# Flamingo block on one core: other engine orders for the first two samples, gate scratch in PSUM, offsets on ScalarE, first context and first w in halves

## The reference

```python
# layernorm of x over its 1024 columns is inp_q; ctx is inp_k and inp_v
t = Wt @ ctx;  p = Wp @ layernorm(x);  g = Wg @ ctx          # 256x256 times 256x1024
att = sum(p * g) over each of 8 groups of 32 rows
y = groupwise Wz @ (att * t)
x1 = x + tanh(g_xattn) * (groupnorm(y) * gn_w + gn_b + ctx)
h = layernorm(x1)
scores = (h @ Wq.T) @ keys.T                                 # 64 experts
gate = softmax of the 16 largest scores, 0 elsewhere
z = h @ A.T                                                  # 512 columns, 8 per expert
out = x1 + tanh(g_ffn) * 2 * ((z * gate) @ B.T)
```

## Time and profile before

| what | us |
|---|---|
| median of three runs | 344.52 |
| profiled execution, its own time | 344.88 |
| span of the profiled execution | 343.1 |
| TensorE busy | 335.0 (98%) |
| VectorE busy | 253.6 (74%) |
| ScalarE busy | 155.2 (45%) |
| GpSimd busy | 155.6 (45%) |

### The profile page before, as it was taken

One profiled execution on the slowest core, in us unless ns is written; L12 is line 12 of the kernel. 1 busy time (PEld: TensorE's weight loads), 2 busy tenths in 40 slices (PEclk: granted clock), 3 DMA queues, 4 the chain that ended last, 5 costly groups with the idle time before them and its releaser, 6 DMA issues.

```text
span 343.1 us, 5733 instructions
## 1 busy us (share of the span) xinstructions
PE 335.0 (98%) x2108; PEld 304.0 (89%) x2108; DVE 253.6 (74%) x656; ACT 155.2 (45%) x254; POOL 155.6 (45%) x148
## 2 busy tenths in 40 slices
PE   8999997999999999999999999999999999999996
PEld 8587997789988999889988899889998899889984
DVE  0858999899688866897868975888668978685362
ACT  2489826873165622554234811656225542144110
POOL 0082999189354470654445381544706544001000
PEclk9999999899999999999999999999999999999999
DMA  8999603660642509052370606424090110002002
GB/s 274 406 394 399 237 1 104 265 214 33 197 171 67 181 6 332 32 166 82 86 283 0 220 29 201 168 71 176 8 330 32 63 62 2 1 0 108 16 32 92
DMA packets 14924, 47.50 MB, mean 138 GB/s; under 512 B 1824, under 2 KB 1952, under 8 KB 14896
## 3 DMA queue, kind: packets, MB, share of 16 engines
q1 hardware_dynamic: 14544, 46.93, 38.5%
q10 hardware_dynamic: 352, 0.20, 0.2%
HBM read 38.74 MB, written 8.39 MB: 137 GB/s over the span
## 4 chain that ended last, share of the span: by engine, by line
PE 86%; POOL 9%; issue 2%; ACT 1%; DVE 1%; POOLq 0%; DVEq 0%
PE z_ps L926 24%; PE w_ps L953 24%; PE w_ps L814 10%; PE w_ps L859 10%; PE t_ps L913 4%; PE z_ps L885 3%; PE w_ps L839 2%; PE z_ps L798 2%; PE w_ps L926 2%; PE w_ps L963 2%; PE t_ps L940 2%; POOL A_lo L267 2%; POOL cT_lo L260 2%; POOL xT_lo L260 1%; POOL B_lo L267 1%
## 5 line engine op out<-in xcount | busy, mean ns | idle before, releaser
L260 POOL TENSOR_TENSOR xT_lo<-xT_in,xT_hi 128x512 fp32r<-128x512 f32 x28 | 35.6, 1295 | 48.9 <-ACT xT_hi L358 46.1
L953 PE MATMUL w_ps<-B_hi,zT_hi 128*128 128x512 f32 x128 | 53.4, 417 | 1.8 <-DVE zT_lo L653 1.8
L953 PE MATMUL w_ps<-B_hi,zT_lo 128*128 128x512 f32 x128 | 51.0, 398 | 0.0
L953 PE MATMUL w_ps<-B_lo,zT_hi 128*128 128x512 f32 x128 | 50.7, 396 | 0.0
L926 PE MATMUL z_ps<-A_hi,hT_hi 128*128 128x288 f32 x224 | 48.5, 298 | 1.0 <-DVE hT_lo L648 1.0
L926 PE MATMUL z_ps<-A_lo,hT_hi 128*128 128x288 f32 x224 | 48.0, 296 | 0.0
L926 PE MATMUL z_ps<-A_hi,hT_lo 128*128 128x288 f32 x224 | 47.9, 296 | 0.0
L437 ACT ACTIVATE ex<-sc,neg_max 128x64 f32<-128x64 f32 x16 | 5.6, 349 | 74.6 <-DVE neg_max L663 74.6
L926 PEld LDWEIGHTS z_ps<-A_hi,hT_hi 128*128 128x128 f32 x224 | 36.3, 189 | 1.8 <-DVE hT_lo L648 1.2
L926 PEld LDWEIGHTS z_ps<-A_hi,hT_lo 128*128 128x128 f32 x224 | 36.1, 189 | 0.0
L260 POOL TENSOR_TENSOR cT_lo<-cT_in,cT_hi 128x512 fp32r<-128x512 f32 x28 | 36.0, 1308 | 0.0
(11 more groups left out here) (147 smaller groups left out, 802.3 us busy)
## 6 DMA issues: line engine op xcount, KB each, us to landing
c_sb<-in_ctx SPq DMA_DIRECT2D x16, 512.0 KB, 4.9
x_sb<-in_x SPq DMA_DIRECT2D x16, 512.0 KB, 7.3
xT_in<-in_xT SPq DMA_DIRECT2D x14, 512.0 KB, 6.7
cT_in<-in_cT SPq DMA_DIRECT2D x14, 512.0 KB, 7.7
out_block<-uw SPq DMA_DIRECT2D x14, 512.0 KB, 2.7
A_in<-in_aT SPq DMA_DIRECT2D x8, 256.0 KB, 12.8
B_in<-in_bT SPq DMA_DIRECT2D x8, 256.0 KB, 12.5
xT_first<-in_xT SPq DMA_DIRECT2D x2, 512.0 KB, 9.0
```

The costliest lines, as they stand in the source:

```text
L260: last = pool.tensor_tensor(lo[:, chunks, :], came[:, chunks, :], hi[:, chunks, :].bitcast(f32), ALU.subtract)
L953: last = pe.matmul(w_ps[k][:, :], z[:, t, row], w[:, j, cols], start=(j == 0 and z is zT_hi and w is B_hi), stop=(j == KN - 1 and z is zT_lo))
```

## The change

- TensorE: `keep_busy(24)` and `keep_busy(8)` become 12 and 4. `first_u` waits for ctx by column halves. In sample 0 the first half of `hT` waits only for the first half of w. `hT(0, 1)` and `hT(1, 1)` move: the one between `out_product(2, 0)` and `out_product(3, 0)`, the other into `z_product(0, 1)`.
- SyncE: ctx of sample 0 is loaded by column halves of both tiles.
- GpSimd: takes lots 0 and 1 ahead of `y_root(0)` and lots 14 and 15 after lots 8 to 11; gives lot 4 away. `x_root(1)` goes ahead of the lots of B, the two `w_root` move by one place or two.
- VectorE: gives lots 0, 1, 14, 15 and `offsets` away and takes lot 4; lots 2 and 3 lie in the wait for `y_root(0)`; w of sample 0 is made in four halves with `hT_low` of its first half between them; half of the row statistics of x of sample 1 lies ahead of `gate(0, 0)`; `x_stats(2)` goes ahead of `hT_low(1, 1)`. The group deviation loses one copy.
- ScalarE: makes the offsets (`offsets`) and for the first two samples a part of the variance (`u_variance`); all eight lots of B and `scale_ctx(1)` come ahead of `exps(1, 0)`.
- The gate's `ex` and `g_rec` lie in columns 288 to 352 of the second z bank in PSUM.

```diff
+        def z_banks(t, n):
+            return w_ps[NH:USES] if t == 1 and n in (0, NB - 1) else z_ps
+
+        def gate_space(t, n):
+            bank = z_banks(t, n)[1]
+            return bank[:, ZH:ZH + NE], bank[:, ZH + NE:ZH + NE + 1]
...
+            def load_first_c():
+                for h in range(NH):
+                    cols = slice(h * HALF, (h + 1) * HALF)
+                    sp.dma_start(c_sb[0][:, :, cols],
+                                 ctx[0].rearrange("t p d -> p t d")[:, :, cols]).then_inc(c_in[h], 16)
...
             x_add(0)
+            lot_low(0)
+            lot_low(1)
             y_root(0)
             pool.wait_ge(w_done, per_tile(0, T - 1))
-            for j in range(KH, KD):
+            for j in range(KH + 1, KD):
                 lot_low(j)
+            w_root(0)
             xT_low(0, 1)
-            w_root(0)
             cT_low(0, 1)
             xT_low(1, 1)
             cT_low(1, 1)
+            x_root(1)
             for j in range(KD, KD + KN):
                 lot_low(j)
-            x_root(1)
+            for j in range(KD + KN + 2, N_LOTS):
+                lot_low(j)
             x_add(1)
             y_root(1)
...
+            def u_variance(n):
+                act.wait_ge(mean_read, n + 1)
+                for t in range(T):
+                    act.activation(att_var[:, T + t:T + t + 1], u_dev[:, t:t + 1], ACT.Identity, scale=u_dev[:, t:t + 1],
+                                   bias=u_mv[:, t, 1:2]).then_inc(u_rows, 1)
+            def offsets(n):
+                act.wait_ge(w_done, per_tile(n, 0))
+                for t in range(T):
+                    act.activation(kappa0[:, t:t + 1], beta[:, t:t + 1], ACT.Identity, scale=-1.0,
+                                   bias=gnb_t[:, t:t + 1]).then_inc(kappa0_done, 1)
+                act.wait_ge(kappa0_done, per_tile(n, T - 1))
+                for t in range(T):
+                    act.activation(kappa[:, t:t + 1], u_dev[:, t:t + 1], ACT.Identity, scale=slope[:, t:t + 1],
+                                   bias=kappa0[:, t:t + 1]).then_inc(kappa_done, 1)
...
             exps(0, 0)
+            offsets(0)
             act.wait_ge(gram_done, per_tile(0, T - 1))
-            for j in range(KD, KD + KN):
+            for j in range(KD, N_LOTS):
                 lot_high(j)
+            scale_ctx(1)
             exps(1, 0)
             zT_high(0, 0)
             cb_copy(1)
-            scale_ctx(1)
             M_high(1)
-            for j in range(KD + KN, N_LOTS):
-                lot_high(j)
+            u_variance(1)
+            zT_high(1, 0)
             residual(0)
-            zT_high(1, 0)
...
-            lot_low(0)
             dve.wait_ge(wg_in, 16)
             att_reduce(0)
-            lot_low(1)
-            slopes(0, lambda: lot_low(2))
-            w_tiles(0)
-            hT_low(0, 0)
-            lot_low(3)
+            def two_lots():
+                lot_low(2)
+                lot_low(3)
+            slopes(0, two_lots)
+            for k in range(NH * T - 1):
+                first_w(k)
+            hT_low(0, 0, (0,))
+            first_w(NH * T - 1)
+            hT_low(0, 0, (1,))
+            lot_low(4)
             u_statistics(1)
             hT_low(1, 0)
-            offsets(0)
+            x_row_stats(0, 1)
             gate(0, 0)
+            x_row_stats(1, 1)
+            x_moments(1)
+            minus_means(1)
...
-            x_stats(1)
-            minus_means(1)
-            gate(1, 0, w_ps[NH:USES])
+            gate(1, 0)
             zT_low(0, 0)
+            lot_low(KD + KN)
             gram_fix(1)
             M_low(1)
             group_deviation(1)
-            for j in range(KD + KN, N_LOTS):
-                lot_low(j)
+            lot_low(KD + KN + 1)
             att_reduce(1)
...
-            keep_busy(24)
+            keep_busy(12)
...
-            keep_busy(8)
+            keep_busy(4)
...
-            out_product(2, 0, lambda: hT(0, 1))
-            out_product(3, 0, lambda: hT(1, 1))
+            out_product(2, 0)
+            hT(0, 1)
+            out_product(3, 0)
             for b in range(1, NB - 1):
                 m = b + 1
-                z_product(0, b)
+                z_product(0, b, (lambda: hT(1, 1)) if b == 1 else None, KN - 2)
```

More of the change, by code:

```diff
@@ L372, in c_high @@
                     act.wait_ge(u_done, per_use(n - 1, USES - 1))
-                act.wait_ge(c_in[n % 2 * T + t], 16 * (n // 2 + 1))
+                if n == 0:
+                    for h in range(NH):
+                        act.wait_ge(c_in[h], 16)
+                else:
+                    act.wait_ge(c_in[n % 2 * T + t], 16 * (n // 2 + 1))
                 act.activation(c_hi[:, t, :], c_sb[n % 2][:, t, :], ACT.Copy,
@@ L460, in _ @@
             M_high(0)
+            u_variance(0)
             act.wait_ge(router_done, 1)
@@ L482, in _ @@
             cb_copy(1)
-            scale_ctx(1)
             M_high(1)
-            for j in range(KD + KN, N_LOTS):
-                lot_high(j)
+            u_variance(1)
+            zT_high(1, 0)
             residual(0)
-            zT_high(1, 0)
-            for h in range(NH):
-                xT_high(h, 2)
-                cT_high(h, 2)
+            xT_high(0, 2)
+            cT_high(0, 2)
+            xT_high(1, 2)
+            hT_high(0, 1)
+            cT_high(1, 2)
             w_square(1)
-            hT_high(0, 1)
             hT_high(1, 1)
+            offsets(1)
             for b in range(1, NB - 1):
@@ L515, in _ @@
                 hT_high(1, m)
+                offsets(m)
             residual(NB - 1)
@@ L545, in x_plus_ctx, with x_row_stats, x_moments @@
                                              ALU.mult, ALU.add).then_inc(xt_done, 1)
[L547 to L551 removed]
+            def x_row_stats(t, n):
+                dve.wait_ge(x_in[t], 16 * (n + 1))
+                for h in range(NH):
+                    step(dve.bn_stats(x_st[:, t, 6 * h:6 * h + 6], x_sb[:, t, h * HALF:(h + 1) * HALF]))
+            def x_moments(n):
                 settle()
@@ L557, in x_stats @@
                 step(dve.tensor_scalar(neg_x[:, :], x_mv[:, :, 0], -1.0, None, ALU.mult))
+            def x_stats(n):
+                for t in range(T):
+                    x_row_stats(t, n)
+                x_moments(n)
             def minus_means(n):
                 dve.wait_ge(c_hi_s, per_tile(n, T - 1))
+                if n > 0:
+                    dve.wait_ge(kappa_done, per_tile(n - 1, T - 1))
                 dve.scalar_tensor_tensor(beta[:, :], c_sum[:, :], ntg[:, 0:1], x_mv[:, :, 0],
@@ L629, in slopes, with first_w @@
                 settle()
+            def first_w(k):
+                t, cols = use(k)
+                dve.wait_ge(u_copied, per_use(0, k))
+                dve.wait_ge(xt_done, per_tile(0, t))
+                dve.scalar_tensor_tensor(uw[0][:, t, cols], uw[0][:, t, cols], slope[:, t:t + 1],
+                                         c_sb[0][:, t, cols], ALU.mult, ALU.add).then_inc(
+                                             w_done if k % NH == NH - 1 else w_half, 1)
             def w_tiles(n):
@@ L636, in w_tiles, with hT_low @@
                                              c_sb[n % 2][:, t, :], ALU.mult, ALU.add).then_inc(w_done, 1)
-            def offsets(n):
-                step(dve.tensor_tensor(kappa0[:, :], gnb_t[:, :], beta[:, :], ALU.subtract))
-                step(dve.tensor_tensor(kappa[:, :], u_dev[:, :], slope[:, :], ALU.mult))
-                settle()
-                dve.tensor_tensor(kappa[:, :], kappa[:, :], kappa0[:, :], ALU.add).then_inc(kappa_done, 1)
-            def hT_low(t, n):
-                for g in range(2):
+            def hT_low(t, n, halves=range(2)):
+                for g in halves:
                     at = (slice(None), t, slice(g * HALF, (g + 1) * HALF))
@@ L654, in zT_low, with gate @@
                                   ALU.subtract).then_inc(zT_lo_s, 1)
-            def gate(t, n, banks=z_ps):
+            def gate(t, n):
+                banks = z_banks(t, n)
+                ex, g_rec = gate_space(t, n)
                 dve.wait_ge(w_rstd, n + 1)
@@ L753, in _ @@
             add_out(2, 0)
+            add_out(3, 0)
+            x_stats(2)
             hT_low(1, 1)
-            add_out(3, 0)
-            offsets(1)
             for b in range(1, NB - 1):
                 m = b + 1
-                x_stats(m)
+                if m > 2:
+                    x_stats(m)
                 minus_means(m)
@@ L777, in _ @@
                 add_out(3, b)
-                offsets(m)
             gate(0, NB - 1)
             zT_low(0, NB - 1)
-            gate(1, NB - 1, w_ps[NH:USES])
+            gate(1, NB - 1)
             add_out(0, NB - 1)
@@ L902, in hT @@
             def hT(t, n):
-                pe.wait_ge(w_done, per_tile(n, t))
                 for g in range(2):
+                    if n == 0 and g == 0:
+                        pe.wait_ge(w_half, t + 1)
+                    else:
```

(4 more changed lines are left out.)

66 lines of the change are left out of this document (33 added, 33 removed).

## The result

Four executions of each kernel on one chip: the kernel before 344.34 us (343.94 to 344.65), the changed one 350.31 (350.01 to 351.63). The ratio is 1.0177, with an interval of 1.0156 to 1.0197. The forecast was 339.7 with 0.94 on faster: wrong, and outside its range of 337.6 to 342.2.

What follows compares the result with a forecast made beforehand. TensorE, busy 335.0 of 343.1 us, was taken as the bound. Terms -1.5 - 1.8 - 1.7 + 0.4 - 0.2 - 0.3 = -5.1, plus 0.3 for thin covers, -4.8: forecast 339.7 us, range 337.6 to 342.2.

Steps and rivals of the forecast that it cites:

- Part 1: Start of TensorE: fewer idle transposes start `first_u` at 7.15 to 7.4, not 8.73; -1.5 us, bounds -2.5 to 0.
- rival 3: TensorE's low clock outlasts the shortened idle products, at `first_u` and `first_gram`; 346 us with 12 us of it; chance 0.06.
- Part 2: `hT(0, 0)`, w in halves: the 0.98 us wait ahead of `z_product(0, 0)` stays; 0, at best -1.0 us.
- Part 3: TensorE's wait for zT_lo ahead of `out_product(0, 0)` goes, -1.8 us, and the half clock behind it, -1.7 us.
- The cover: Margin in zT_lo's arrival: ready at 53.4 against TensorE's request at 54.1, 0.7 us.
- Part 4: GpSimd's chain after w of sample 0: +0.4 us at `gram(1)`, -0.2 us at `hT(0, 1)`.
- The +0.4 for `gram(1)`: TensorE waits 0.4 us in `gram(1)` for the last low parts of the transposes, ending at 49.1 on GpSimd.
- the +1.5: Upper end for the change in TensorE's wait ahead of `hT(0, 1)`, forecast at -0.2 us; lower end -0.34.
- Part 5: The rest: `hT(0, 1)` placed between products, -0.3 us; offsets on ScalarE and waits after 69 us, 0.
- rival 2: GpSimd, stretched by collisions, becomes what the first samples wait for; `hT(0, 1)` waits 2 us more; 341.7 us, chance 0.10.
- Rival 1: The zT_lo wait only shrinks and the half clock returns; some 2.3 us won, 342.2 us; chance 0.13.
- rival 4: Better: no new wait around zT_lo or GpSimd, and the 0.98 us wait gone too; 338.1 us or less, chance 0.12.

Runs made afterwards that it cites:

- e10: The kernel before with only the start changed, 12 and 4 idle transposes for 24 and 8; 344.27 us, ratio 0.9991 over twelve executions.
- e13: e11 with 24 and 8 idle transposes at the start, as in the kernel before; 340.76 us, ratio 0.9896.
- e14: e11 timed again, with the short start of 12 and 4 transposes, beside e13; 340.82 us, ratio 0.99.
- e7: e5 with the gate's exponentials and reciprocal back in SBUF instead of PSUM; 340.73 us, ratio 0.99.
- e8: e5 with 24 and 8 idle transposes at the start, as in the kernel before; 342.41 us, ratio 0.9931.
- e5: Changed kernel; GpSimd waits for VectorE's low part of lot 12 after its lot 11, and for that of lot 13 ahead of `x_add(1)`; 341.82 us, ratio 0.9922.
- e12: Changed kernel; GpSimd waits ahead of its lot 10 for `gate(1, 0)`, before lot 12 is asked for; 341.67 us, ratio 0.9929.
- e1: Changed kernel; VectorE's low part of lot 12 reads one input from PSUM instead of SBUF (wrong values, same size); 345.19 us, ratio 1.0033.
- e2: Changed kernel; one statistics operation of about 0.6 us reading PSUM alone put ahead of lot 12 on VectorE; 350.33 us, no ratio given.
- e6: Changed kernel; low part of lot 12 made in four 128x128 subtractions, no gap for GpSimd; 351.07 us, ratio 1.0164.
- e9: Changed kernel; a 128x2 addition with both inputs in SBUF put directly ahead of lot 12 on VectorE; 350.63 us, ratio 1.0188.
- e4: Changed kernel; lot 12 moved behind `group_deviation(1)` on VectorE, next to lot 13; 346.58 us, no ratio given.
- e3: Changed kernel; GpSimd waits once, for VectorE's low part of lot 12, before going on to lots 14 and 15; 342.9 us, ratio 0.9932.
- e11: e5 with w of sample 0 made by whole tiles and its low parts behind it, as before the change; 341.64 us, ratio 0.9904.

## Why the prediction was wrong, point by point

**Part 1, the start: right in place, wrong in worth.** `first_u` starts at 6.90 (7.15 to 7.4 forecast), 1.83 earlier. But the -1.5 isn't kept. In e10 the ratio is 0.9991 where -1.5 would be 0.9957, just outside its interval, and e13 against e14 gives nothing either. The mechanism of rival 3, the clock, was right in kind; I looked for it at `first_u` and in a slow level left over from the start. It came at 24 us, as a fall from the full level, and by the two groups of times in about half of the executions. The slow transposes at the start, which I took for the low clock, are not shown to be that: the windows of both kernels have a granted clock of 1.00 over the first 10 us, with 224 ns a transpose before and 235 after. The profiled execution of the changed kernel itself shows 1.00 there and kept its 1.8. The loads of ctx, which I took at 0 and had landed at 6.0, set a floor: `first_u` waited for them 1.13 us in e14 and started at 7.02, and 0.90 in e7 and started at 6.83, so fewer idle products would win nothing more.

**Part 2, hT(0, 0): right on the wait, a term mis-sized.** The wait is still 0.98 us, to the hundredth. The halves of w I took at 0; e8 against e13 shows +1.2, by way of what the prediction mentions and hardly charges: `first_w(3)` stands behind the first `hT_low` and makes GpSimd's chain late. `x_add(1)` starts at 59.62 in e8 and at 58.35 in e13, and the wait ahead of `hT(0, 1)` is 1.3 us in the one and gone in the other.

**Part 3, zT_lo: right.** It was to be ready at 53.4 against a request at 54.1; it starts at 53.06 and ends at 53.74, and `out_product(0, 0)` starts at 53.91 without a wait and at the full clock. The cover was 0.2 us, where I had 0.7. The -1.8 came, and of the -1.7 1.5: the 12 products take 2.98 us for 4.46. The scratch in PSUM stopped the collisions of the gate and was, as said, worth nothing beyond the cover (e7).

**Part 4, GpSimd: its times are right, what it does to VectorE isn't priced.** I reckoned `x_add(1)` to its end at about 62.4, and it ends at 62.35. No lot of GpSimd was held up by much. The +0.4 for `gram(1)` did not come; nothing waits there. `hT(0, 1)` lost its wait, but only since everything came later; in e5 it waits 0.7, within the +1.5, and in e12 1.6.

**Part 5: right.** The transposes of `hT(0, 1)` and `hT(1, 1)` take 0.87 each for 1.09 and 1.05, -0.4 for the -0.3, and TensorE waits for nothing after 69 us.

**The step that failed** lies between Parts 3 and 4: what lot 12 costs VectorE ahead of M_lo stands in no term of the sum, which puts it at 0 without a reason. The prediction says of the low parts that the two engines now make side by side that they "hold each other up, which counts in rival 2", and rival 2 is a GpSimd stretched by collisions. It never asks what one new VectorE instruction in that stretch costs VectorE, though the diff puts one right ahead of `gram_fix(1)`, M_low and so `n_product(1)`. By my own rows its price would have been up to 1.3 us, the worst of the earlier trace rows. At that price it would have changed little. The measured price is 9.24, of which 7.9 us became a wait of TensorE and brought some 2.9 us of half clock behind it. The highest value of 16 in a trace is not a bound where the mechanism is a queue behind another engine's stream; the bound was that stream's length, and both of its ends stood in the prediction: zT_low ends at 53.4 in Part 3 and `x_add(1)` at 62.4 in Part 4, 9.0 us. A second thing: the kernel before had lots 12 to 15 behind `group_deviation(1)`, and they never met the stream. The row of its VectorE timeline:

```profile
61.09 2.49 DVE L536 TENSOR_TENSOR B_lo<-B_in,B_hi 128x512 fp32r<-128x512 f32 x4
```

By the earlier trace rows GpSimd's stream ended at 55.96 + 5.00 = 60.96 there, 0.13 us ahead of them, so the old trace had no row of such a lot against it. That VectorE came so late was luck, which the change took away.

Two smaller sums of the prediction are off, and neither bears on this. Rival 1 wins 2.4 less the 0.3 added back, which is 2.1 and not 2.3; and rival 4 with the bound of Part 1 is 338.1 - 1.0 = 337.1, not the 337.6 at the lower end of the range.

By the Trainium skill, "SBUF — State Buffer", Who interferes with whom, whoever issues first holds the shared pair for its whole instruction and the other is blocked. That agrees with e1 (one input in PSUM: 0.68 us) and with the waits up to 1.3. By this rule alone lot 12 would have gone in at the end of the instruction of GpSimd under way, within 1.25 us, and the forecast would have stood. The runs show seven instructions of GpSimd going ahead of it; the measurement decides.

**The sum, with what was measured.** To the end of `z_product(0, 1)`: start -1.7 (`zT(0, 0)` at 46.81 for 48.51), zT_lo -1.8, its half clock -1.5, the wait ahead of `hT(0, 1)` -0.3, its transposes -0.4, the new wait +7.9, the half clock behind it about +2.9. That is +5.1, and 5.15 was measured. Take the last two away and -5.7 is left. e13, which has the old start, should then end `z_product(0, 1)` 5.7 - 1.7 = 4.0 earlier than the kernel before, and does so by 3.96. e5, where the new wait is gone but for 0.6, ends it 2.3 earlier (78.90): 1.6 of the start's gain went to the half clock near 24 us, 0.6 to M_lo and 0.7 to the wait for w. In the medians e5 keeps 3.2 and e13 3.3.

**What stays open.** What decides whether a VectorE instruction gets in at GpSimd's next border or only at the stream's end. In the changed kernel itself three tiny operations got in within 1.33 us at 45.7 to 48.8, in the same unbroken stream, 5 us before lot 12 did not. Two of them are `TENSOR_SCALAR` with a single tensor input in SBUF (`x_ve` 0.61, `neg_x` 1.33 us), so one input less does not by itself keep every operation from being held up. Right behind them a full-sized operation with both inputs in SBUF got in as well, while GpSimd's `x_root(1)` beside it took 1.25 us for 0.70 before:

```profile
48.74 0.69 DVE L805 TENSOR_TENSOR Wp_lo<-Wp_in,Wp_hi 128x512 fp32r<-128x512 f32 x1
```

Phase (e2) and size (e6, e9) are ruled out, and another place in VectorE's order (e4) doesn't help. A stop of GpSimd at or shortly before the request cures it in the profiled execution of every kernel that has one (e3, e5, e7, e8, e11 to e14), and one execution each of e2 and e4 escapes without one, for a reason that no trace shows. What goes on between the engines in such a stop was not tried further.

## What to carry to other kernels

An instruction of VectorE with both inputs in SBUF, asked for while GpSimd runs a line of instructions without a gap, can cost the rest of that line whatever its size; price it at the line's length, not at the worst row of the trace, and keep it off the path of the bounding engine. If it must stand there, give it one input in PSUM, or put a wait of half a us into GpSimd's stream just before it: here that gave back 7.4 to 8.6 us in the medians (e3, e5, e12), and made TensorE wait 0.5 to 1.6 us for GpSimd's later results. Time a shortened warm-up of TensorE in ten executions, not in one: it may come out in two groups, of which a single profile shows one.

## What the runs showed of the hardware that was not expected

- 8.71 us for an addition on 128x2, and 9.24 for a subtraction on 128x512, against 0.68 with one input in PSUM: VectorE was passed over until GpSimd's stream ended, in the latter case for 7 instructions in a row.
- A GpSimd stop of 0.74 us that ended 0.43 us before the request was enough for two lots to get in later (1.39 and 1.09 us).
- In e10 TensorE's clock fell from 2.4 to 1.2 GHz near 24 us with no idle time around it, in a stretch with 16 products of 16x64; by their times and mean granted clocks about half of the executions of e10 and e14 have it, 2.6 to 2.8 us apart from the others.
